# The query projection of a tile moved from the start of a step to the end of the step before it, in a six-layer attention and feed-forward kernel

## The reference, cut to what matters

```python
for i in range(DEPTH):                       # 6 layers
    x = attn_layer(shift_tokens(x), Wqkv[i], q_scale[i], k_scale[i], Wo[i]) + x
    x = ffn_layer(shift_tokens(x), ln_g[i], ln_b[i], W1[i], b1[i], W2[i], b2[i]) + x

# attn_layer
q, k, v = split(x @ Wqkv)                    # 16 heads of 64 each: 1024 columns each
q = l2norm(q) * qs ; k = l2norm(k) * ksc     # t / max(norm(t), 1e-12)
q = q * cos * scale + rotate_half(q) * sin * scale
k = k * cos / scale + rotate_half(k) * sin / scale
out = softmax(mask(8 * q @ k.T)) @ v         # windows of 32, each sees itself and the one before
return out @ Wo

# ffn_layer
xn = layernorm(x) ; a, gate = split(xn @ W1 + b1)
return a * gelu(gate) @ W2 + b2
```

## Time and profile before

| | us |
|---|---|
| median of 3 runs | 2007.84 |
| the three runs | 2007.84, 2001.0, 2007.87 |
| the profiled execution | 2001.63 |
| its span | 1999.8 |
| PE busy | 1771.6 (89%) |
| DVE busy | 1543.1 (77%) |
| POOL busy | 1454.8 (73%) |
| ACT busy | 1156.1 (58%) |

### The profile page before, as it was taken

How to read it: one execution, slowest core, us unless ns; L and a number is a source line. 1 busy time by engine, 2 the same in 40 slices (tenths; PEclk the granted TensorE clock), 3 DMA queues, 4 the chain that set the end, 5 groups by cost and what they waited for, 6 DMA issues and landing times. The chain is left out here.

```text
span 1999.8 us, 85355 instructions
## 1 busy us (share of the span) xinstructions
PE 1771.6 (89%) x34184; PEld 1277.4 (64%) x34184; DVE 1543.1 (77%) x2729; ACT 1156.1 (58%) x1966; POOL 1454.8 (73%) x967
## 2 busy tenths in 40 slices
PE   7764789999999999999999999999999999999995
PEld 3453466666666666666666666666666666666664
DVE  4774798778878877788788777887887788778864
ACT  2311456666666666666666666666666666666663
POOL 3221787787788778877887787778777877887771
PEclk9985899999999999999999999999999999999998
DMA  4000222223232223222223322233222232322220
GB/s 151 2 3 1 56 63 57 64 60 84 66 74 58 54 55 94 63 68 58 63 56 85 76 67 55 52 81 81 62 58 62 61 86 63 74 60 52 55 63 22
DMA packets 93581, 123.43 MB, mean 62 GB/s; under 512 B 27760, under 2 KB 41808, under 8 KB 93392
## 3 DMA queue, kind: packets, MB, share of 16 engines
q1 hardware_dynamic: 93232, 122.42, 24.3%
q10 hardware_dynamic: 288, 0.13, 0.0%
HBM read 20.74 MB, written 1.05 MB: 11 GB/s over the span
## 5 line engine op out<-in xcount | busy, mean ns | idle before, releaser
L999 POOL TENSOR_TENSOR across<-unit,turns 128x1024 f32<-128x1024 f32 x192 | 497.4, 2591 | 275.5 <-issue 265.6
L1006 POOL TENSOR_TENSOR rotated<-along,across 128x1024 f32<-128x1024 f32 x192 | 495.7, 2582 | 14.2
L1155 DVE TENSOR_REDUCE sums<-squares 128x16 f32<-128x1024 f32 x192 | 234.0, 1219 | 177.9 <-ACT squares L1054 177.7
L1246 PE MATMUL turn<-identity,rotated 128*128 128x128 f32 x1536 | 204.7, 276 | 35.5 <-POOL rotated L1006 34.3
L1246 PEld LDWEIGHTS turn<-identity,rotated 128*128 128x128 f32 x1536 | 172.3, 141 | 98.0 <-issue 82.5
L1032 POOL TENSOR_TENSOR along<-unit,turns 128x1024 f32<-128x1024 f32 x96 | 228.0, 2375 | 0.0
L1350 PE MATMUL proj_a<-w_qkv,shift_a 128*128 128x512 f32 x384 | 189.5, 616 | 36.3 <-DVE unit L1180 30.1
L1114 ACT COPY val<-proj_a 128x1024 f32<-128x1024 f32 x96 | 97.2, 1012 | 180.7 <-PE proj_a L1350 180.7
L1379 PE MATMUL att<-o_t,w_o 128*128 128x128 f32 x1536 | 188.9, 277 | 0.0
L1278 PE MATMUL proj_a<-w_qkv,shift_a 128*128 128x512 f32 x384 | 184.4, 603 | 5.0 <-POOL shift_a L989 3.7
L1379 PEld LDWEIGHTS att<-o_t,w_o 128*128 128x128 f32 x1536 | 181.0, 193 | 1.0 <-issue 1.0
(11 more groups left out here) (201 smaller groups left out, 3366.2 us busy)
## 6 DMA issues: line engine op xcount, KB each, us to landing
v_win<-val SPq DMA_DIRECT2D x1536, 64.0 KB, 2.0
w_qkv<-wqkv_dram SPq DMA_DIRECT2D x18, 512.0 KB, 3.9
w_o<-wo_dram SPq DMA_DIRECT2D x6, 512.0 KB, 4.7
where<-positions_dram SPq DMA_DIRECT2D x1, 2048.0 KB, 10.7
w_ffn<-ffn_dram SPq DMA_DIRECT2D x12, 170.5 KB, 2.3
w_ffn<-ffn_dram SPq DMA_DIRECT2D x6, 192.0 KB, 2.3
x_tok<-x_dram SPq DMA_DIRECT2D x4, 256.0 KB, 4.2
out_dram<-final SPq DMA_DIRECT2D x4, 256.0 KB, 2.4
```

Of the source, the lines that this page charges most:

```text
L999: pool.tensor_tensor(a[:, :, ::-1, :], u, table, ALU.mult).then_inc(acrossed[j], 1)
L1006: pool.tensor_tensor(rotated[j][:, :, :], along[j][:, :, :], across[j][:, :, :], ALU.add).then_inc(rotated_in[j], 1)
L1155: dve.tensor_reduce(sums[:, j, :], squares[j][:, :, :], AX.X, ALU.add).then_inc(summed[j], 1)
L1246: mm = pe.transpose(bank[:, TILE * (i % 4):TILE * (i % 4) + TILE], buffer[:, TILE * i:TILE * i + TILE], identity[:, :])
```

## The change

Q of tile `p + 1` (written as `s + 2`) is done at the end of step `s`, behind the output projection and, in an even step, ahead of widen. Q of tile 0 stands ahead of the first step. On ACT, the squares of the queries stand first in a step, ahead of the gelu and of `p_t`; on DVE, their sum stands first, ahead of the mass and of `hidden`. The loop has 43 rounds in place of 44, and one more pair of steps is written out.

```diff
-        FIRST, ROUNDS = 7, 44
+        FIRST, ROUNDS = 7, 43
@@ scalar, step
+                    if live["p"]:
+                        square(0)
                     if live["down"]:
                         act.wait_ge(down_in, (layer_of(s - 5) + 1) * 32)
@@
                     if live["p"]:
-                        square(0)
                         square(1)
@@ vector, step
+                    if live["p"]:
+                        sum_squares(0)
                     if live["b"]:
                         dve.wait_ge(weighed, 2 * b + 2)
                         after(dve, mass_inverted, b)
@@
                     if live["p"]:
-                        sum_squares(0)
                         sum_squares(1)
@@ tensor
+                def project_queries(m, parity):
+                    pe.wait_ge(shifted, 2 * m + 2)
+                    pe.wait_ge(q_in, (layer_of(m) + 1) * 16)
+                    after(pe, v_laid, m)
+                    stand_alone(pe, passed)
+                    for half in range(2):
+                        mm = pe.matmul(bank_a[:, half, :], shift_a[parity][:, :], w_qkv[:, 512 * half:512 * half + 512],
+                                       start=True, stop=True)
+                    mm.then_inc(q_projected, 1)
@@ tensor, step
                     if live["p"]:
+                        pe.wait_ge(k_in, (layer_of(p) + 1) * 16)
                         pe.wait_ge(shifted, 2 * p + 2)
-                        pe.wait_ge(q_in, (layer_of(p) + 1) * 16)
-                        after(pe, v_laid, p)
-                        stand_alone(pe, passed)
-                        for half in range(2):
-                            mm = pe.matmul(bank_a[:, half, :], shift_a[mine][:, :], w_qkv[:, 512 * half:512 * half + 512],
-                                           start=True, stop=True)
-                        mm.then_inc(q_projected, 1)
-                    if live["p"]:
-                        pe.wait_ge(k_in, (layer_of(p) + 1) * 16)
                         after(pe, united[1], p)
@@
                         mm.then_inc(attended, 1)
+                    if live["next"]:
+                        project_queries(s + 2, odd)
                     if live["up"]:
                         pe.wait_ge(normed_f, h + 2)
@@
+                project_queries(0, 0)
                 run(pe, step)
```

## The result

The changed kernel takes 2057.5 us (median of 4 runs, 2052.8 to 2062.7), against 2005.7 us for the kernel before in the same comparison: a ratio of 1.0262, with a 95% interval of 1.0228 to 1.0297. It is slower by 52 us. The forecast was 2060, in a range of 2034 to 2084.

A forecast was written before the change was run, and what follows sets the result against it. No engine is full; joints bound the loop through PE's list before the mixing and a DVE stretch. 45 x (1.51 - 0.26) = 56.3, less 2, on 2001.63 gives 2055.9, put at 2060; range 2034 to 2084 us.

The forecast's parts named there:

- The loop and its count: PE's list from V to mixing, then DVE's stretch, sets the loop; a pair's gain or loss counts about 45 times.
- The delay of K: Odd step: K waits for the third `hidden`, queued on DVE behind sum, mass and reciprocal; 1.51 us longer.
- Everything behind K keeps its distances.: Odd step: squares and sum of the keys follow K, and `heads_out` follows the mixing, at unchanged distances.
- Table load as second path: ACT, odd step: 1.28 us load behind the squares, hidden behind DVE's queue; alone it would delay K by 0.7 us.
- Rival 3: ACT's table switch costs more than its row: 0.5 us a pair more, 2083 us; chance 0.04.
- The even step's 0.26 us: Odd to even step: K 0.78 us earlier, but POOL's rotated keys limit V's gain to 0.26 us.
- Rival 1: Even step: POOL's chain doesn't hold V, so the whole 0.78 us is gained; 2033 to 2041 us; chance 0.09.
- rival 2: Odd step: `gated` comes before PE needs it, K starts 0.32 us earlier; 1982 us; chance 0.04.
- The first steps: First five steps, without gelu: Q can run while PE waits for the exponential; 2 us gained in all.
- The sum: Whole kernel: 45 x (1.51 - 0.26) = 56.3, less 2, is 54.3 us on 2001.63: 2055.9, put at 2060.
- two levels: Three runs of the kernel before lie at 2001.0 and 2007.8 us; the forecast was put 4 us higher.
- Rival 4: PE's new 1.83 us idle time in each pair lowers the clock: 58 us more, 2118 us; chance 0.03.

The follow-up runs named there:

- experiments five and six: Q moved at odd steps' end only: with POOL's power behind the rotated keys 1995.9 us; POOL's table product behind the root 2032.0 us; both 1968.3 us.
- experiment five: POOL's power moved behind the rotated keys: changed kernel 2061.8 us; kernel before 2012.3 us; kernel with Q moved at odd steps' end only 1995.9 us.

## Why the prediction was right

- *The loop and its count.* Right: 45 waits of K for the gating, all but two at full clock. In the usual case a pair loses 1.04 us (37.50 - 36.46), where 1.25 was forecast.
- *The delay of K* (1.51 us forecast). Measured 1.66. Q's start, squares, sum, mass and reciprocal came at the distances taken from the rows within 0.02 us. The gating stood 0.32 us behind the reciprocal in place of 0.22, and K 0.15 behind the gating in place of 0.10.
- *"Everything behind K keeps its distances."* This step was wrong, and it made the forecast of a pair too high: K to V is 8.82 us, 0.37 less than the 9.19 of before. `heads_out` starts 4.26 us behind K in place of 4.49 (the mixing took 1.49 us in place of 1.62; why is open), and root up to `unit` takes 2.02 us in place of 2.17: it no longer meets POOL's copies, and its third operation (L92) takes 0.19 us in place of 0.31. In the kernel before it ended 0.04 us behind such a copy:

```profile
1035.86 0.31 DVE L92 TENSOR_TENSOR root_work<-inv_norm 128x32 f32<-128x32 f32 x1
```

```profile
1035.84 0.29 POOL L989 COPY shift_a<-xa 64x128 f32 x1
```

So the odd step is 1.28 us longer (19.89 - 18.61), not 1.51.
- *Table load as second path.* Right in order and size: 0.64 us late by ACT alone (0.7 forecast), 1.28 us for the load, started 0.02 us after the squares' end. Rival 3, a dearer switch, is excluded by these rows: the gelu starts 0.01 us behind the load, and no drain shows.
- *The even step's 0.26 us.* Measured 0.24, but the reason given was half of it. I had POOL's keys as what holds V; they do, yet `unit` stands within 0.11 us of the same place, since the root moved under POOL's table product. Taking either away alone gives nothing (experiments five and six), both together 0.46 us. Rival 1, a gain of 0.78 us, did not come; rival 2, a K that finds the gating done, is excluded by the 45 waits.
- *The first steps*, -2 us forecast, were 3.2 us longer, and the clock had a part in them: 0.93 granted from 230 to 320 us, where the kernel before has 1.00 from 220 to 310. In the other kernels these six steps take 103.9 to 109.0 us (103.65 before, 106.87 after), so one execution of each can't tell what the change does to them.
- *The sum.* That 2057.5 lies so near 2060 is in part luck. The pairs were forecast at 56.3 us and took 51.4, of which 3.6 are the clock's (below), so the mechanism forecast was worth about 48. The first steps came out 5 us above their term, the tail 2.8 us below. The 4 us added for "two levels" have no ground: the fourth run of the kernel before took 2003.61 us, and 31 later ones spread from 1998.8 to 2015.3 without a gap.
- *Rival 4, the clock.* It exists, but rarely. K behind the wait took 1.95 us at full clock in nearly all steps; twice it took longer:

```profile
350.98:354.31 3.33, 3.33 (x4) 1.16 (x5) 0.00 (x0) 0.00 (x0) 2.85 (x3) 0.53 0.36 83
918.99:920.83 1.84, 1.84 (x9) 1.51 (x8) 0.54 (x1) 1.50 (x2) 0.94 (x4) 0.50 0.26 62
1030.71:1032.50 1.79, 1.79 (x4) 0.78 (x5) 0.00 (x0) 0.00 (x0) 1.79 (x2) 1.00 0.39 95
```

(Stretch, length, engines, granted clock third from the end.) In the first two stretches the granted clock was at or near its lower level, 1.2 GHz. The first is K itself, right behind a wait of 2.18 us; the second begins 2.37 us after a K that had waited 1.93 us, and over that K the clock was 0.75. In the third, a K behind the same wait of 1.93 us, it was at its upper level, 2.4 GHz. These two steps were 21.84 and 21.50 us in place of 19.89, 3.6 us in all. The changed kernel with the power's move (experiment five) has the same wait and four such steps, of 21.4 to 21.8 us; no other kernel's trace has one between V 8 and V 96. Why these and not the others is open.

## What to carry to other kernels

When an operation is moved forward in one engine's list, look at what its followers then do at the head of theirs: a short operation placed early, whose input comes late, stops everything behind it, and the price is what hangs on the last of these. The move on PE was worth some 10 us, its two companions on ACT and DVE cost some 60; no one was waiting for their results at the new place. And where a wait can be shortened, look for the second chain that ends at the same time before expecting the gain.

## What the runs showed of the hardware

A DVE operation with two SBUF sources and a POOL product do not run side by side: the one that comes second waits until the other has ended. In the kernel before, the odd step's `along` came while POOL's `rotated` (1043.68 to 1046.04) was running:

```profile
1045.13 1.98 DVE L1233 TENSOR_TENSOR along<-unit,turns 128x1024 f32<-128x1024 f32 x1
```

```profile
1045.98 3.35 POOL L999 TENSOR_TENSOR across<-unit,turns 128x1024 f32<-128x1024 f32 x1
```

It ended 1.07 us after that `rotated`, and POOL's next product, begun meanwhile, took 3.35 us in place of 2.35. The three lengths of `along` are one length: 1.40, 1.98 and 3.36 us are what was left of the POOL product running at its start (0.31, 0.91 and 2.28 us), and 1.08 us more. So it is in all 88 `along` of DVE between V 8 and V 96 of the kernel before: each ends 1.08 or 1.09 us after that product. The POOL product begun meanwhile ends 2.21 to 2.24 us after `along`, in all 88. A 128x32 root operation of 0.19 us takes 0.69 beside a table product of 0.73 and ends 0.04 us after it. Reductions of squares (one SBUF source) and `unit` (a PSUM source) keep their 1.21 to 1.23 us throughout.

The Trainium skill ("SBUF — State Buffer", SBUF: two separate sides) says so: the port pair shared by VectorE and GpSimd is an exclusive lock held for a whole instruction, and among others a VectorE operation with two SBUF inputs takes part, against a GpSimd operation that reads SBUF. The runs agree in all these rows.

Moving one 0.73 us product out of the way was worth 28 us in one kernel (1995.9 and 1968.3, ratios 0.9959 and 0.9815), 12 us in the kernel before, and cost 34 us in a third (1997.9 and 2032.0, ratios 0.9960 and 1.0127), where it let POOL's next products start sooner and fall on `along`.
